# One block for preparation and scores, experts turned, a guess in column tiles, and seams without their own blocks

## The reference

```python
bias = sign(pos) * log1p(abs(pos))            # pos: pixel minus key, 1024 x 64 x 2 for each of 16 heads
bias = relu(bias @ cpb_w1 + cpb_b1)           # 2 -> 32
bias = relu(bias @ cpb_w2 + cpb_b2)           # 32 -> 32
sim = q @ k.T + (bias @ cpb_w3 + cpb_b3)      # then softmax and values, projection, MLP
```

## Time and profile before

| | |
|---|---|
| timed runs, median of 3 | 1770.22 us (1770.0 to 1770.23) |
| profiled execution | 1775.4 us, span 1773.6 us |
| busy: PE, DVE, ACT, POOL | 1535.2, 886.6, 852.8, 317.3 us |
| PE, share of the span | 87% |
| mean granted clock of PE | 0.939 |
| data moved | 69.63 MB |

### The profile page before, as it was taken

How to read it: one execution, slowest core, us unless ns; L and a number is a source line. 1 busy time by engine, 2 the same in 40 slices (tenths; PEclk the granted TensorE clock), 3 DMA queues, 4 the chain that set the end, 5 groups by cost and what they waited for, 6 DMA issues and landing times. The chain is left out here.

```text
span 1773.6 us, 29966 instructions
## 1 busy us (share of the span) xinstructions
PE 1535.2 (87%) x12396; PEld 772.9 (44%) x12396; DVE 886.6 (50%) x1357; ACT 852.8 (48%) x1161; POOL 317.3 (18%) x135
## 2 busy tenths in 40 slices
PE   6689999999677978999999997999999999448598
PEld 4222222222333755566566565654444444126254
DVE  2468888888733535776777774010001000357242
ACT  3467777777343444677777764122222222231521
POOL 0466666665210001000000000000000000020000
PEclk9589999999898987999999998999999999779889
DMA  1000000000020004343444420000000000000000
GB/s 61 1 2 2 2 2 2 3 2 2 1 77 15 1 1 166 136 156 131 161 167 167 149 102 1 1 0 1 0 1 0 0 0 0 29 0 4 1 0 24
DMA packets 20658, 69.63 MB, mean 39 GB/s; under 512 B 688, under 2 KB 17072, under 8 KB 18096
## 3 DMA queue, kind: packets, MB, share of 16 engines
q1 hardware_dynamic: 20240, 66.73, 10.1%
q10 hardware_dynamic: 288, 1.05, 0.2%
HBM read 33.17 MB, written 34.60 MB: 38 GB/s over the span
## 5 line engine op out<-in xcount | busy, mean ns | idle before, releaser
L489 POOL TENSOR_TENSOR l_work<-l_a_scores,l_work 128x2048 f32<-128x2048 f32 x64 | 233.0, 3642 | 129.7 <-PE banks L607 115.8
L1777 PE MATMUL banks<-s_h,pack_l2f_l3f 128*128 128x512 f32 x512 | 221.0, 592 | 0.0
L1804 ACT ACTIVATE s_h<-banks,pack_l2f_l3f 128x512 f32<-128x512 f32 x128 | 88.0, 688 | 241.8 <-PE banks L1777 175.7
L547 DVE TENSOR_TENSOR l_work<-banks,sc_negc 128x1024 f32<-128x1024 f32 x128 | 156.3, 1221 | 49.7 <-PE banks L654 32.8
L607 PE MATMUL banks<-l_work,pack_l 32*32 32x512 f32 x4096 | 159.8, 607 | 23.4 <-ACT l_work L509 19.7
L509 ACT ACTIVATE l_work<-banks,pack_l 128x1024 f32<-128x1024 f32 x128 | 142.7, 1114 | 76.2 <-PE banks L607 75.4
L1370 PE MATMUL banks<-pack_l2a,r_e 128*128 128x128 f32 x1024 | 142.6, 282 | 26.3 <-ACT r_e L1422 26.3
L1422 ACT ACTIVATE r_e<-banks,r_max 128x1024 f32<-128x1024 f32 x128 | 142.5, 1113 | 44.9 <-DVE r_max L1463 44.8
L1457 DVE TENSOR_REDUCE r_raw<-banks 128x1 f32<-128x640 f32 (+1 forms) x128 | 109.5, 856 | 104.6 <-PE banks L1351 104.6
L1777 PEld LDWEIGHTS banks<-s_h,pack_l2f_l3f 128*128 128x128 f32 x512 | 97.3, 190 | 122.5 <-issue 122.5
L1351 PE MATMUL banks<-r_k,r_q 32*128 32x128 f32 (+3 forms) x832 | 147.9, 464 | 1.1 <-DVE r_v L1295 1.1
(11 more groups left out here) (380 smaller groups left out, 2142.8 us busy)
## 6 DMA issues: line engine op xcount, KB each, us to landing
distances<-r_rd SPq DMA_DIRECT2D x16, 2048.0 KB, 6.3
r_band<-distances SPq DMA_DIRECT2D x16, 1536.0 KB, 7.0
pack_l2f_l3f<-pack_dram_l2f SPq DMA_DIRECT2D x1, 2212.5 KB, 10.2
pack_l2f_l3f<-pack_dram_l3f SPq DMA_DIRECT2D x1, 1248.5 KB, 5.3
pack_l<-pack_dram_l SPq DMA_DIRECT2D x1, 1093.0 KB, 6.4
residual<-x ACTq DMA_DIRECT2D x2, 512.0 KB, 7.6
out<-residual SPq DMA_DIRECT2D x2, 512.0 KB, 3.1
pack_l2a<-pack_dram_l2a SPq DMA_DIRECT2D x1, 715.0 KB, 4.7
```

Of the source, the lines that this page charges most:

```text
L489: pool.tensor_tensor(image(H1R[:, c % 3]), bc(a, 2, 16), bc(b, 3, HW), ALU.add).then_inc(sem("added"), 1)
L547: dve.tensor_tensor(image(H2M[:, (2 * c + part) % 3]), image(PS[:, MAX + j:MAX + j + 2]), bc(NEGC[:, j:j + 2, n, i, rows(half)], 3, HW), A ...
L1777: ins = pe.matmul(bank, W["w2"][:, col:col + P], H1[:, c, m], start=(m == 0), stop=(m == HB - 1))
L1804: act.activation(H[:, c, k], PS[:, g % 8], ACT.Tanh, bias=bias).then_inc(sem("tanh"), 1)
```

## The change

- **Seams.** `Stage.clear` goes. A stage leaves itself in `Stage.past`, and POOL clears its semaphores at the end of its own program in the next stage's block. `send` and `ready` are called by SP inside the stages' blocks. A last block clears what the experts leave.
- **Start.** The first pack goes in two pieces: the columns up to `kw` (ident moved among them), then the rest. There is no loading block; the loads are issued within the first stage, and three engines wait for the rest where they need it.
- **Preparation and scores in one block** (`l0_bias`). POOL's first additions may start before the preparation has ended. DVE takes the units 0 to 10 alone; ACT takes the first layer's A part of units 11 to 15 and the B part of 14 and 15. The units are spread differently over the samples.
- **Guess.** The two halves of the second layer go to partitions 0 to 63 and 64 to 127 of one bank, in two column tiles; one tanh does both; L1684's products use two row tiles; ACT does one of the two copies.
- **Experts.** Hidden units are output rows now. The selection is four column tiles; the transposes of the hidden units go; the weights are spread over the hidden units by a product with a 0/1 matrix (`gates`, four row tiles), ACT does the relu, DVE multiplies, and `values` sums in four banks. Three of eight groups of hidden units are made before the weights are needed. The result is written per 512 tokens inside the block.

```diff
-    def clear(self):
-        with self.nc.Block() as block:
+    def block(self):
+        block = self.ctx.enter_context(self.nc.Block())
+        self.ctx.callback(Stage.clear_past, block)
+        return block
...
+    def clear_past(block):
+        past, Stage.past = Stage.past, None
+        if past:
             @block.gpsimd
             def _(pool):
-                for s in self.sems.values():
+                for s in past.sems.values():
                     pool.sem_clear(s)
...
+LOOPED = 12
+WITH_SAMPLE = (2, 1, 2, 1, 1, 1, 1, 1)
+A_ON_ACT = (11, 12, 13, 14, 15)
+B_ON_ACT = (14, 15)
-        A_ON_ACT = (3, 7, 11, 13, 14, 15)
...
             for c in range(8):
                 hat(c)
-                if c in (1, 3, 5):
-                    a_out(2 * c + 1)
+        for u in range(LOOPED - 1, UNITS):
+            a_out(u)
+            if u in B_ON_ACT:
+                b_out(u)
...
+        offsets(0)
+        pe.wait_ge(sem("vt_out"), 2)
+        pe.wait_ge(sem("vm"), NB)
+        pe.wait_ge(sem("km"), NB)
+        offsets(1)
...
-                    pe.matmul(PS[0:N, 1 + h, 0:HALF_H], W["to_nodes"][N:N + 32], W["to_steps"][N:N + 32, h * HALF_H:(h + 1) * HALF_H],
-                              start=True, stop=False, tile_position=(N, 0))
+                    pe.matmul(PS[N * h:N * h + N, 1, 0:HALF_H], W["b2_lift"][N:N + 32],
+                              W["to_steps"][N:N + 32, h * HALF_H:(h + 1) * HALF_H], start=True, stop=False,
+                              tile_position=(N, N * h), skip_group_check=True)
...
+                        ins = pe.matmul(PS[N * h:N * h + N, 1, 0:HALF_H], H1[:, m], W["w2"][:, c:c + HALF_H], start=False,
+                                        stop=(m == HB - 1), tile_position=(0, N * h), skip_group_check=True)
...
+                act.activation(H2[:], PS[:, 1, 0:HALF_H], ACT.Tanh).then_inc(sem("h2"), 1)
...
+                        ins = pe.matmul(PS[:, 3 + h, j * N:j * N + N], H2[half, j * P:(j + 1) * P],
+                                        W["ident" if last else "to_nodes"][half], start=True, stop=True,
+                                        tile_position=(N * h, 0))
...
+            def hidden(j, chunks):
+                for n in chunks:
+                    if AHEAD <= j:
+                        pe.wait_ge(sem("gated"), NCH * (j - AHEAD) + n + 1)
+                    elif j:
+                        pe.wait_ge(sem("kept"), NCH * (j - 1) + n + 1)
+                    pe.matmul(PS[:, n], W["keys"][:, j * P:(j + 1) * P], XN[:, n * CH:(n + 1) * CH], start=True, stop=True
+                              ).then_inc(sem("hidden"), 1)
...
+            for j in range(EB):
+                gates(j)
+                if j:
+                    values(j - 1, low)
+                if j + AHEAD < EB:
+                    hidden(j + AHEAD, every)
+                if j:
+                    values(j - 1, high)
+            values(EB - 1, every)
```

More of the change, by code:

```diff
@@ L29 @@
 class Stage:
+    past, count = None, 0
     def __init__(self, nc, ctx):
[L33 to L34 removed]
+        self.nc, self.ctx, self.sems, self.number = nc, ctx, {}, Stage.count
+        Stage.count += 1
+        ctx.callback(self.leave)
     def sb(self, name, shape, dt=F32):
@@ L1593, in l2f_pack @@
     row[0] = 1.0
-    p.add("to_nodes", np.concatenate([nodes, row * np.ones((1, NB * NODES), np.float32)]))
+    p.add("to_nodes", np.tile(nodes, (2, 1)))
+    p.add("b2_lift", np.concatenate([np.zeros_like(nodes), row * np.ones((1, NB * NODES), np.float32)]))
     steps = np.tile(integration(NODES, np.arange(PIX) * DT), (NB, 1))
@@ new lines, in values @@
+            def values(j, chunks):
+                for n in chunks:
+                    pe.wait_ge(sem("gated"), NCH * j + n + 1)
+                    ins = pe.matmul(PS[:, ACC + n], W["values"][:, j * P:(j + 1) * P], HT[:, j, n], start=(j == 0),
+                                    stop=(j == EB - 1))
+                    if j == EB - 1:
+                        ins.then_inc(sem("out"), 1)
+            every, low, high = range(NCH), range(2), range(2, NCH)
+            select()
+            hidden(0, low)
@@ new lines, in _ @@
+            pe.wait_ge(sem("scores"), 1)
+            turn(TURNED, lambda t: SELT[:, t * P:(t + 1) * P], "turned")
+            hidden(0, high)
+            for j in range(1, AHEAD):
+                hidden(j, every)
+            pe.wait_ge(sem("weights"), 1)
+            turn(GATES, lambda t: GW[:, 4 * t:4 * t + 4].rearrange("p n e -> p (n e)"), "turned_back")
+            pe.wait_ge(sem("spread"), NCH)
+            pe.wait_ge(sem("gates_out"), 1)
+            for j in range(EB):
[6 more added lines that the diff above has]
+                    values(j - 1, high)
@@ L2332, in _ @@
+            for j in range(AHEAD, EB):
+                for n in range(NCH):
+                    kept(j, n)
+        @block.gpsimd
+        def _(pool):
+            for n in range(NCH):
+                own = W["ident"][quarter(n), quarter(n)]
+                pool.tensor_copy(SPREAD[quarter(n)], bc(own, 2, EH)).then_inc(sem("spread"), 1)
         @block.vector
@@ L2445, in build, with mlp_ready, pack @@
+                def mlp_ready(sp):
+                    sp.wait_ge(arrived["mlp"], 16)
+                l0_attend(nc, X, PS, W, SALL, VT, mlp_ready)
+        def pack(name, tile):
+            return Weights(tile, offsets[name])
+        l2a, l2f = sb("pack_l2a", [P, columns("l2a")]), sb("pack_l2f_l3f", [P, columns("l2f", "l3f")])
         with ExitStack() as l1:
             tile = l1.enter_context(nc.sbuf_tensor("pack_l1", [P, columns("l1")], F32))
-            send({"l1": tile, **stay})
-            l0_mlp(nc, X, PS, ready("mlp", shared))
@@ L2463, in build @@
+        l2_trajectory(nc, X, PS, pack("l2f", l2f), W, l3a_ready)
+        W = pack("l3a", shared)
+        layer_norm(nc, "l3a_norm", X, XN, PS, W["centre"], W["mean"], W["eps"], send_l3f)
+        l3_attention(nc, X, XN, PS, W, l3f_ready)
+        W = pack("l3f", l2f)
         layer_norm(nc, "l3f_norm", X, XN, PS, W["centre"], W["mean"], W["eps"])
-        l3_experts(nc, X, XN, PS, W)
-        dump(X)
+        l3_experts(nc, X, XN, PS, W, out_dram, stored)
+        with nc.Block() as block:
+            Stage.clear_past(block)
```

1194 lines of the change are left out of this document (609 added, 585 removed).

## The result

The changed kernel takes 1706.26 us (median of four runs, 1703.56 to 1709.64) where the one before, on the same chip, took 1770.22 (1770.0 to 1770.25). The ratio is 0.964, with an interval of 0.9619 to 0.9661: 64 us, 3.6%, less. The forecast was 1705.5.

A forecast was written before the change was run, and what follows sets the result against it. No single engine's total decides: TensorE is busy 87% of 1773.6 us, and all engines meet at each seam. Gains 2.4 + 7.3 + 3.1 + 20 + 17 + 14 + 0.9 = 64.7 us took 1770.22 to 1705.5; range 1692 to 1722.

The forecast's parts named there:

- Sampling loop: Convolution to kv: with the units spread differently, the samples end at 67.9, 7.3 us less; bounds 10.9 and 2.
- clock rival: Rival A: the shortened guess leaves TensorE too thin, the clock falls in guess and experts, 1725 us; chance 10%.
- Start: Kernel start to the convolution: a smaller first piece brings the convolution to 15.1, 2.4 us gained; bounds 0 and 2.9.
- kv to scores: From kv to the end of the offsets: 13.4 us instead of 16.5, gain 3.1; bounds 1 and 6.
- Seams: Between stages: clearing blocks, empty blocks and sends leave the path, 20 us gained; bounds 17 and 22.
- Guess: Guess of the trajectory, eight rounds: two column tiles run at once, 17 us gained; bounds 20 and -4.
- rival B: Guess and experts' gates: tiles run in turn, the guess gains nothing and gates are slow, 1731 us; chance 6%.
- C: Experts and guess: the drain is paid at tiling switches, 3 and 5 us, 1713; with small misses to 1722, 17%.
- Rival A: Guess and experts: the clock falls, +3.5 us a round in half the rounds, +5 in experts, 1725 us; chance 10%.
- Experts: From the last seam to the last add: 71.7 us instead of 85.7, gain 14; bounds 20 and 5.
- End: Last add to the kernel's end: 0.9 us gained, with a landing of up to 3.1; bounds -0.5 and 2.
- Rival D: Sweep loop: a changed guess element forces a second sweep, 343 us more, 2050 us in all; chance 2%.

The follow-up runs named there:

- the sized version: Changed kernel plus four expert steps ahead and unread full-array products sized to idle time in norms, gates, and in and ahead of the sampling loop: 1694.26 us, ratio 0.9564.
- the last experiment: The sized version: changed kernel plus unread products fitted to idle time and four expert steps ahead; 1694.26 us, ratio 0.9564.

## Why the prediction was right, and where it wasn't

The total came within 1 us, but by two errors that cancel: 6.3 us too much for the sampling loop, and 6.9 us gained in stages for which nothing was forecast. That they are of one size is luck.

**Sampling loop: the term that failed.** The step read "per step one or two layer-1 units at 1.05 us". That is half of the 2.09 us that two units take together. A unit uses two of the four row tiles, so two run side by side; alone, one takes 2.08 us. The new division is mostly lone units, so PE's step is 3.02 us, above GpSimd's 2.35, and PE became the bound: 1.0 us gained of 7.3. The signs named for this term failed with it: kv came at 71.66, not at 65 to 66, and the first products of the scores at 91.92, not near 86. The lone price was in the trace of before, hidden in a group with an outer wait (3.33 us for two units, the second of which had to wait for its bank). In the end the plan itself was sound at the other clock level: at 1.00 a lone unit takes 1.13 us, and the sized version reached kv in 48.8 us; the forecast, 50.4 (67.9 less 17.5).

**Stages that I left as they are: 6.9 us gained.** The prediction gave the untouched stages no change, and its clock rival only a loss. The MLP takes 29.35 us in ten of the eleven profiles with short seams and 32.5 to 32.7 in the two with clears of their own, so the shorter seam goes with its start at the high clock. It isn't the whole condition: with the old division of the units, short seams too, the clock fell in the third us of the MLP, and it took 31.33. The norm's 3.1 us are the clock as well, in its first six records. Before, in the changed kernel and with separate clears:

```profile
648.31 5.46 PE L1088 MATMUL banks<-residual,pack_l2a 128*128 128x512 f32 x6 [3.48 <-PEq L2403]
629.19 2.81 PE L1174 MATMUL banks<-residual,pack_l2a 128*128 128x512 f32 x6 [1.09 <-PEq L940]
640.84 2.81 PE L1180 MATMUL banks<-residual,pack_l2a 128*128 128x512 f32 x6 [3.10 <-PEq L55]
```

PE had stood idle for 3.48 us there, and for 3.10 with separate clears, where the clock was still up; that is why they didn't take this gain back. The rest isn't pinned down: the heads moved between 407.7 and 414.7 us over runs in which their code is the same.

**Start: right size, and the path as forecast.** L250 begins at 5.05 (forecast 4.9), the second half of x lands by 8.88 (8.4), and chunk 2 starts at 11.47 (11.0). But the forecast missed that L250 would get shorter by 1.4 us of itself, so that with one transfer most of the gain is there too, and that the clock moves the start of the convolution by 2 us from run to run. L250's 2.22 us stood in the earlier trace rows, and I didn't ask why it was so long. The forecast's own terms from 11.0 on add up to 14.9, not 15.1.

**kv to scores**, 3.1, as computed: 13.4 us from kv to the end of the offsets.

**Seams** 21.3 for 20: 0.26 to 0.30 us each, 0.54 and 1.26 ahead of the sweep and behind it. At no other seam does anything show of GpSimd's late clears, not at the end of the gates either (0.30).

**Guess** 16.6 for 17, the round 6.82 for 6.8: the factor of 2 for two column tiles was right to 6% (3.67 to 1.95), rival B is refuted, and the price of C isn't seen: by the Trainium skill's "TensorEngine Tiling (Array Packing)", Key Properties, a mode change drains the engine; here L1764 follows L1757's start by 0.58 us and takes the time of its records. Rival A is not refuted but held off, as the run without the unread products showed.

**Experts** 12.5 for 14: the weights were there 1.6 us sooner than computed (gates at 15.0 for 16.6), the full steps took 8.13 for 8.0 us and the last ones 4.7 for 4.5, but the first took 8.0 for 6.0, 1.8 of it in the products around 1650 at the low clock. What brought the clock down there stays open, since behind the same three waits it stayed up in one kernel with four steps ahead and fell in the other (5.40 us again in the last experiment). The terms of the forecast add up to 54.9 from the gates on, not 55.1.

**End** 1.7 for 0.9: a quarter of the result at a time lands in 2.0 us, not in 3.1.

**Rival D** didn't happen: SP's wait for the sweep is one of 345.0 us, for 345.1 in the earlier trace rows.

## What to carry to other kernels

Price a tiled product by how many of its tiles are filled when it runs: a product that pairs with its neighbour in the trace has a lone price of its own, and a new order that separates them pays it. Where a stage ends with TensorE idle, the next one's first microseconds may run at half speed; unread full-array products that end before the idle time does were free here, and with more of them in and ahead of the sampling loop the kernel got 14 us faster, 3.9 of them in the gates and chunks and 7.8 in the loop. The same products sized up to 1.5 times the idle time cost 10. When the total is right, check the terms: here 6 us too much in one and 7 too little in others made it so.

## What the runs showed of the hardware

- A loop of row- and column-tiled products stood at a granted clock of 0.50 with PE busy 10.00 of 10.00 us; one full-array product of 256 or 384 columns per step went with 1.00, though not from the first step on in two of three kernels.
- The guess with PE busy 17.86 of 20 us without its unread products: 0.51; with them (18.55 of 20): 1.00.
- The same six records behind an idle PE: 5.46 us behind 3.48 us of idle time, 2.81 behind 3.10 and behind 1.09.
- A VectorE operation of 128x1024 took 2.22 us beside a memset on GpSimd, and 0.81 without.
- A float32 product shows as two records; eleven products of 512 columns back to back took 9.71 us (22 records), 0.88 each.
